# Out product, residual and norm of cross-attention in 28 tiles of 128 rows, and the first context load moved

## What is computed

```python
x = layernorm(x + self_attention(x))            # 16 heads of 32, causal
q = x @ Wq.T + bq; k = ctx @ Wk.T + bk; v = ctx @ Wv.T + bv
x = layernorm(x + softmax(q @ k.T) @ v)         # one head of 512
c = scan over the 16 batches of a gated recurrence (sigmoid, sigmoid, tanh)
x = layernorm(x + tanh(x @ wo.T + c_final @ uo.T + bo))
```

## Time and profile before

| | |
|---|---|
| median of 3 runs | 1415.57 us |
| profiled execution | 1416.02 us, span 1414.1 us |
| TensorE busy | 1385.4 us (98%), mean granted clock 0.994 |
| VectorE, ScalarE, GpSimd busy | 921.9, 731.6, 569.7 us |
| DMA | 157.94 MB, 37.8% of 16 engines' time |
| self-attention | about 0 to 385 us |
| cross-attention | about 385 to 837 us, 28.5 us per batch in the middle |
| recurrence and output gate | about 837 to 1414 us |

### The profile page before, as it was taken

The page is one execution under the profiler, slowest core; times in us unless marked ns, Lnnn a source line. Parts: engine busy times, 40 slices in busy tenths (PEclk is TensorE's granted clock), DMA queues, the critical chain, the costliest instruction groups (busy, mean ns, idle before and its releaser), DMA issues.

```text
span 1414.1 us, 28483 instructions
## 1 busy us (share of the span) xinstructions
PE 1385.4 (98%) x10017; PEld 1211.0 (86%) x10017; DVE 921.9 (65%) x1911; ACT 731.6 (52%) x1989; POOL 569.7 (40%) x475
## 2 busy tenths in 40 slices
PE   7999999999999999999999999999999999999997
PEld 4677777777789999999999988999999999999775
DVE  4589989999657756776677663345453444536697
ACT  4488888888565566656665655222232222222232
POOL 2476767676476565656565620000000000010264
PEclk9999999999999999999999999999999999999999
DMA  7014323335366675667567953010010100000353
GB/s 212 25 56 107 104 75 81 104 104 156 109 172 215 200 240 182 204 195 233 188 205 213 210 155 112 1 27 13 13 26 0 26 13 19 31 1 31 101 186 123
DMA packets 133079, 157.94 MB, mean 112 GB/s; under 512 B 62304, under 2 KB 70496, under 8 KB 133008
## 3 DMA queue, kind: packets, MB, share of 16 engines
q1 hardware_dynamic: 133008, 157.01, 37.8%
HBM read 105.61 MB, written 35.78 MB: 100 GB/s over the span
## 4 chain that ended last, share of the span: by engine, by line
PE 64%; issue 3%; POOL 3%; DMA 1%; DVE 1%; ACT 1%; POOLq 0%; ACTq 0%; DVEq 0%
PE banks L1522 16%; PE banks L1551 11%; PE banks L1007 9%; PE banks L1023 8%; PE banks L1036 6%; PE banks L1553 6%; PE banks L992 5%; POOL o_r L2097 1%; PE banks L977 1%; DMA s_cx_raw<-in_cx 1%; PE banks L1983 1%; PE banks L1053 1%; POOL o_rstd L2105 1%; POOL x_cx_lo L1367 1%; PE banks L2014 0%
## 5 line engine op out<-in xcount | busy, mean ns | idle before, releaser
L461 ACT ACTIVATE s_p<-banks,a_nmax 112x224 f32<-112x224 f32 (+1 forms) x512 | 198.1, 412 | 60.0 <-DVE a_nmax L572 59.9
L759 POOL TENSOR_TENSOR s_p<-s_p,a_rinv 112x896 f32<-112x896 f32 (+1 forms) x128 | 164.5, 1306 | 118.9 <-DVE a_rinv L580 115.8
L1496 POOL CAST m_hi<-w_raw 128x2048 fp32r<-128x2048 f32 x1 | 2.3, 2266 | 407.8 <-PE banks L1522 407.8
L1639 ACT ACTIVATE f_gate<-f_gate 128x448 f32<-128x448 f32 x90 | 52.2, 580 | 198.6 <-DVE f_gate L1762 198.6
L1759 DVE TENSOR_TENSOR f_gate<-banks,f_xg_early 128x448 f32<-128x448 f32 x45 | 28.1, 624 | 189.6 <-PE banks L1553 189.6
L1367 POOL TENSOR_TENSOR x_cx_lo<-s_cx_raw,x_cx_hi 125x512 fp32r<-125x512 f32 x96 | 120.8, 1296 | 37.0 <-ACT x_cx_hi L1136 37.0
L571 DVE TENSOR_REDUCE a_nmax<-banks 112x1 f32<-112x224 f32 x256 | 97.9, 382 | 24.5 <-PE banks L277 23.7
L461 ACT ACTIVATION_READ_ACCUMULATOR s_p<-banks,a_nmax 112x1 f32 x512 | 111.6, 218 | 0.0
L294 PEld LDWEIGHTS banks<-identity,s_p 112*112 112x112 f32 x768 | 88.0, 134 | 21.8 <-issue 2.3
L294 PE MATMUL banks<-identity,s_p 112*112 112x112 f32 x768 | 105.4, 261 | 1.2 <-POOL s_p L759 0.7
L1360 POOL TENSOR_TENSOR s_ct<-s_ct_raw,s_ct 128x750 fp32r<-128x750 f32 x60 | 98.6, 1669 | 0.0
(11 more groups left out here) (255 smaller groups left out, 3727.5 us busy)
## 6 DMA issues: line engine op xcount, KB each, us to landing
s_ct_raw<-in_ct SPq DMA_DIRECT2D x16, 1500.0 KB, 6.7
s_cx_raw<-in_cx SPq DMA_DIRECT2D x16, 1500.0 KB
a_xt<-in_xt SPq DMA_DIRECT2D x16, 448.0 KB, 6.3
a_xrow<-in_x SPq DMA_DIRECT2D x16, 448.0 KB, 5.9
a_xres<-in_x SPq DMA_DIRECT2D x16, 448.0 KB, 6.7
x_scratch<-a_xn SPq DMA_DIRECT2D x16, 448.0 KB, 3.3
x_scratch<-x_xn SPq DMA_DIRECT2D x16, 448.0 KB, 4.6
x_halves<-x_halves SPq DMA_DIRECT2D x16, 448.0 KB, 3.2
```

The costliest lines, as they stand in the source:

```text
L461: e = act.activation((p1 if c else p0)[:, g, h, :], src, ACT.Exp, bias=nmax[:, g % 2, c, h:h + 1], accum_out=rsum[:, g % 2, c, h:h + 1])
L759: pool.tensor_tensor(p[:, g, :, :], p[:, g, :, :], inv, ALU.mult).then_inc(norm_done, 1)
```

## The change

Four batches are 896 rows, which is 7 tiles of 128. The out product, the residual, the norm and the stores of x2 and of its halves work on these tiles: after batch 0 of four (q = 0) one tile is complete, after batches 1, 2 and 3 two more each. `ot_hi` and `ot_lo` are 384 columns wide and hold the remainder of a batch until the next. The row sums' reciprocals are laid out by 112 rows and are needed by 128, so they are stored to memory and loaded back; the residual's rows are loaded from memory by 128 rows as well, and POOL adds the bias in place. All loops of the stage run over four batches instead of two.

```diff
 # tables and the two new loads (SP)
+        OF = ((0, 1), (1, 3), (3, 5), (5, 7))
+        SLOT = ((0,), (1, 2), (0, 1), (2, 0))
+        PUT = (((0, T, 0),), ((0, 160, T), (160, T, 0)), ((0, T, 64),), ((0, 96, 288), (96, T, 0)))
...
+            def inverse_rows(b, at, odd):
+                i, q = four(at)
+                wait(sp, rinv_stored, 16 * (b + 1))
...
+                    sp.dma_start(rinv_rows[:, odd, 0:rows(at)], rinv_dram[i][128 * OF[q][0]:128 * OF[q][1]].rearrange("(n p) -> p n", p=128))\
+                      .then_inc(rinv_in, 16)
+            def residual_rows(b, at):
+                wait(sp, rinv_done, b + 1)
...
+                    sp.dma_start(rinv_scratch[b].rearrange("(c p) -> p c", p=R), rinv[:]).then_inc(rinv_stored, 16)
+                wait(sp, r_done, TC * b)
+                sp.dma_start(x1b[:, 0:rows(at), :], tiles_of(x1_rows, at)).then_inc(x1b_in, 16)
...
+            def loads(b, odd, at=None):
+                i, q = four(b if at is None else at)
+                if within(b - 2, B):
+                    inverse_rows(b - 2, (i, q - 2), odd)
...
+                residual_rows(b - 1, (i, q - 1))
 # out product (PE)
-                for c in rows:
+                for c in some[0:n]:
+                    slot = slice(128 * SLOT[q][c], 128 * SLOT[q][c] + 128)
...
-                            mm = pe.matmul(ps_h[0:R, c, :], y[:, k, c * R:c * R + R], w[:, k, :],
-                                           start=(i == 0), stop=(i == 3 * KC - 1))
+                            mm = pe.matmul(ps_h[:, c, :], y[:, k, slot], w[:, k, :], start=(i == 0), stop=(i == 3 * KC - 1))
 # exponentials (ACT): x1th(b + 1) goes between the two halves
+                    if c == 1 and within(b + 1, B) and not (isinstance(b, int) and b == 0):
+                        x1th(b + 1)
...
-                if within(b + 1, B) and not (isinstance(b, int) and b == 0):
-                    x1th(b + 1)
 # residual (DVE)
+                wait(dve, rinv_in, 16 * (b + 1))
 # bias of the residual (POOL)
-                wait(pool, x1_in[odd], 16 * (i + 1))
-                wait(pool, r_done, TC * (b - 1))
+                wait(pool, x1b_in, 16 * (b + 1))
...
+                if within(b - 1, B):
+                    residual_bias(b - 1, (i, q - 1))
                 if within(b, B):
                     cxl(b)
 # self-attention's SP: the first context load stands ahead of the loop over batches 4 to 13
+            sp.dma_start(shared.ct_raw[:], io["ct"][0].rearrange("(k p) t -> p k t", p=128)).then_inc(shared.ct_in, 16)
+            sp.dma_start(shared.cx_raw[:], io["cx"][0].rearrange("(c p) d -> p c d", p=XR)).then_inc(shared.cx_in, 16)
             with sp.Fori(2, B // 2 - 1) as i:
...
             step(B - 2, B % 2)
-            sp.dma_start(shared.ct_raw[:], io["ct"][0].rearrange("(k p) t -> p k t", p=128)).then_inc(shared.ct_in, 16)
-            sp.dma_start(shared.cx_raw[:], io["cx"][0].rearrange("(c p) d -> p c d", p=XR)).then_inc(shared.cx_in, 16)
```

More of the change, by code:

```diff
@@ L948, in sync @@
                 loads(b, b % 2)
[L949 to L952, removed]
+            with sp.Fori(1, B // 4 - 1) as i:
+                for q in range(4):
+                    loads(4 * i + q, q % 2, (i, q))
+            for b in range(B - 4, B - 1):
+                loads(b, b % 2)
             for i, name in enumerate(("wi_t", "wf_t")):
@@ L1074, in step, with separate @@
                 if isinstance(b, int) and b == B - 1:
-                    out(b - 1, range(0, 1))
+                    out(b - 1, b - 1, range(0, 1))
                 elif within(b - 1, B):
-                    out(b - 1)
+                    out(b - 1, (i, q - 1))
             for b in range(4):
[L1080 to L1085, removed]
+                step(0, b)
+            with pe.Fori(1, B // 4 - 1) as i:
+                for q in range(4):
+                    step(i, q)
+            for b in range(B - 4, B + 1):
+                step(b // 4, b % 4)
             for t in range(6):
                 next_input(t)
-        def separate(act, b):
+        def separate(act, b, at=None):
+            n = rows(b if at is None else at)
             wait(act, xn_done, TC * (b + 1))
             wait(act, halves_stored, 16 * b)
-            act.activation(halves[:], xn[:].bitcast(U16).rearrange("p c (d w) -> p c w d", w=2), ACT.Copy).then_inc(halves_done, 1)
+            act.activation(halves[:, 0:n, :, :], xn[:, 0:n, :].bitcast(U16).rearrange("p c (d w) -> p c w d", w=2), ACT.Copy)\
+               .then_inc(halves_done, 1)
         def scalar(act):
@@ L1129, in oth @@
                     wait(act, ot_done, 2 * b + half + 1)
-                    act.activation(ot_hi[:, 2 * half:2 * half + 2, :], ps_g[:, half, 0:2 * T], ACT.Copy).then_inc(oth_done, 1)
+                    for first, end, place in PUT[q]:
+                        a = act.activation(ot_hi[:, 2 * half:2 * half + 2, place:place + end - first], ot_columns(half, first, end), ACT.Copy)
+                    a.then_inc(oth_done, 1)
             def cxh(b):
@@ L1138, in exp @@
             def exp(b):
+                if isinstance(b, int) and b == 0:
+                    act.wait_ge(shared.xn_done, TC * B)
                 wait(act, pt_done, XC // 2 * b)
@@ L1193, in scalar @@
             x1th(1)
-            act.wait_ge(shared.xn_done, TC * B)
-            for b in range(2):
-                step(b)
-            with act.Fori(2, B - 2) as b:
-                step(b)
-            step(B - 2)
-            step(B - 1)
-            step(B)
+            act.wait_ge(shared.r_done, TC * B)
+            for b in range(4):
+                step(0, b)
+            with act.Fori(1, B // 4 - 1) as i:
+                for q in range(4):
+                    step(i, q)
+            for b in range(B - 4, B + 1):
+                step(b // 4, b % 4)
             next_columns(0)
@@ L1266, in statistics @@
+            def statistics(b, at):
+                n = rows(at)
+                each = TC // n
+                for c in range(n):
+                    wait(dve, r_done, TC * b + each * (c + 1))
+                    dve.bn_stats(stats[:, c, :], r[:, c, :]).then_inc(stats_done, each)
+                for c in range(n):
                     dve.wait_ge(pad_done, 1)
-                    wait(dve, stats_done, TC * b + c + 1)
-                    dve.bn_aggr(mv[:, c, :], stats[:, c, :]).then_inc(mv_done, 1)
@@ L1313, in step @@
                 if within(b - 1, B):
-                    residual(b - 1, 1 - odd, range(0, 1) if isinstance(b, int) and b == B - 1 else range(TC))
-                if within(b, B) and not (isinstance(b, int) and b == B - 1):
+                    residual(b - 1, (i, q - 1), range(0, 1) if isinstance(b, int) and b == B - 1 else range(TC))
+                if within(b, B):
                     inverse(b)
@@ L1385, in gpsimd @@
             for b in range(4):
[L1386 to L1391 removed]
+                step(0, b)
+            with pool.Fori(1, B // 4 - 1) as i:
+                for q in range(4):
+                    step(i, q)
+            for b in range(B - 4, B + 2):
+                step(b // 4, b % 4)
         opening.separate, opening.store = separate, store
```

238 lines of the change are left out of this document (131 added, 107 removed).

## The result

The changed kernel takes **1527.38 us** (median of 4 runs, 1525.30 to 1529.19) against 1415.39 before: 1.0785 times, 95% interval 1.0763 to 1.0807. That is 112 us more, where 32 were forecast, and outside the range.

The account below looks back on a forecast made before the run. TensorE, busy 98% of the span, was taken to bound the kernel, with a ring through the DMA queue near its limit. 1416.0 + 19 (cross-attention) + 13 (self-attention) = 1448 us, range 1420 to 1466.

Parts of the forecast that it names:

- the standstill in self-attention: Self-attention, batch 5: columns land late behind the moved context load, POOL held 15 us, TensorE idle 12; +13 us (9 to 17).
- the gain: Out product in cross-attention: 28 tiles of 128 rows instead of 32 of 112, 48 products fewer, 11.2 us saved.
- the ring through the residual's rows: Cross-attention: next context load waits for POOL's subtractions, these for the bias, that for the residual's rows; 29.4 us a step.
- The forecast's second ring: Cross-attention: SP waits for the reciprocals' store, delaying transposed columns, ACT's rounding and exponential, then TensorE's transposes; 29.4 us.
- the slack: Cross-attention: transposes start 4.9 us after the context rows' issue, which was to carry the first two steps.
- the two weights: Cross-attention's last context load: two 1 MB weights ahead of it in the queue, no longer hidden; 5 us.
- the draining: Last step of cross-attention: POOL's subtractions end later; 3 us (0 to 4.9).
- The store is 224 values of 4 bytes: Cross-attention: the reciprocals' store behind `s_ahead` in the queue delays what follows by 0.3 us (0 to 1.1).
- Slower still: Rival: TensorE's clock falls in each step's wait, up to 1.7 us in 12 steps; 1468 us, chance 0.13.
- The faster rival: Rival: ring and standstill both hidden, residual's rows landing within 17.8 us of the context rows' issue; 1405 us, chance 0.09.
- The fit beside it: The skill's rule, one DMA takes 2.0 us plus bytes over 436 GB/s: halves would land after 3.1 us, not 11.8.
- the moved load: Self-attention: the first context load, now directly ahead of batch 5's columns in the queue, makes them late; +13 us.

Follow-up runs that it names:

- e5: The kernel before with only the first context loads of cross-attention issued ahead of self-attention's loop; 1429.86 us.
- e12: The kernel before with each context rows' load split in two, 112 and 13 of its 125 partitions; 1412.74 us.
- e8: e6 with each context rows' load split in two, 112 and 13 of its 125 partitions; 1401.18 us.
- e2: The change with the reciprocals copied from SBUF to SBUF, nothing of them through memory; 1453.08 us.
- e6: e2 with the first context loads back at their old place and POOL adding the bias behind the context's low parts; 1411.18 us.
- e1: The change without the reciprocals' store, load and waits, the product multiplied by 1.0 instead; 1454.11 us.
- e4: The change with each reciprocal stored as 4 bytes, 512 bytes from one address to the next; 1452.29 us.
- e9: The change with each reciprocal stored as 4 bytes, 64 bytes from one address to the next; 1453.62 us.
- e3: The change with each reciprocal stored with 127 zeros behind it, as one piece of 512 bytes; 1456.95 us.
- e11: The change with each store of reciprocals issued a second time, to another scratch; 1606.11 us.
- e10: The change with the two reciprocals of a partition stored side by side, 112 writes of 8 bytes a batch; 1472.16 us.

## Why the prediction was wrong

**Right: the standstill in self-attention**, +13 forecast, +14 measured alone (e5), with POOL held 15.42 us (15) and TensorE 12.2 (12) in the profile after.

**Right: the gain**, 11.2 us forecast, 10.8 to 11.6 between e12 and e8. It only appears once nothing else is in the way: by the context loads, a one-tile step takes 26.2 us in e8 against 28.5 in e12, and a two-tile step 28.5 in both.

**Right in its mechanism, too small in its size: the ring through the residual's rows.** The forecast has 19.4 + 2.4 + 7.55 + 0.1 = 29.4 us for every step. Without dense writes e2 shows 20.3 + 2.37 + 8.38 = 31.1 in a two-tile step (its context rows at 618.13, the rows below on POOL), and 27.5 to 29.3 in the one-tile steps, on average 30.16:

```profile
638.43 2.40 POOL L1426 TENSOR_TENSOR x_x1b<-x_x1b,s_bv_all 128x1024 f32<-128x1024 f32 x1 [10.31 <-DMA x_x1b<-x_scratch]
640.80 8.38 POOL L1440 TENSOR_TENSOR x_cx_lo<-s_cx_raw,x_cx_hi 125x512 fp32r<-125x512 f32 x6
```

e6 shows the mechanism: in cross-attention only POOL's order changed against e2, and the ring was gone. The forecast's second ring, through SP's wait for the store, wasn't the limit: e1 and e2 are without it and no faster than e4 and e9.

In time, cross-attention without the dense writes is 1453.1 - 1415.4 - 14 = +24 us; +19 was forecast, with 30 as the bound. That the two are so near is partly luck. By the context loads of e2 and before, the later twelve steps cost 21 us more (30.3 each against 28.5), where the forecast has 11, and the first two 9, where it lets the slack carry them. What follows the last context load is 2 us shorter, where the forecast adds 5 for the two weights and 3 for the draining: the step that holds the weights takes 30.7 us, no more than the two-tile steps before it.

**Wrong: "The store is 224 values of 4 bytes. I take 0.3 us (bounds 0 and 1.1)."** With its reading back it cost 5.0 us a step (35.20 less 30.16), 74 us in all (1527.4 less 1453.1), about seventeen times the value taken and over four times the bound; 4.1 of them lie in the store's own flight. I had bounded it by the nearest row that counts bytes, a 448 KB DMA, because no row of the kernel before shows a store of many small pieces side by side. A bound by bytes can't hold what isn't paid by the byte; and the store wasn't one DMA more in the queue, it slowed the DMAs that were in flight. Where such a store is free, the runs lie 4 to 9 us over the forecast's sum of 1448 and inside its range: e2, e3, e4 and e9 take 1452 to 1457.

**The rivals.** "Slower still" had the right sign and the wrong cause: the clock did fall (0.91 over 440 to 800), but behind waits that the writes made. TensorE's own work is 305.54 / 360 x 35.20 = 29.9 us a step there and 340.44 / 360 x 30.16 = 28.5 in e2, so at most 1.4 of the 5.0 us can be the clock's; whether these lie on the path stays open. The faster rival needed the residual's rows at 17.8 us; in e2 they are ready at 20.3. The fit beside it (the Trainium skill, DMA: Bandwidth & Descriptors, Anatomy of one DMA) is stated for DMAs that GpSimd issues, and here SP issues all of them; e2's halves, at 16.9 us, are as far from its 3.1 as those of rows 5.

One remark of the forecast's gain is wrong and moves nothing: both layouts have 3584 rows of output and none in padding; what falls is the number of tiles, by four.

**The parts of the 112 us:** 74 dense writes, 14 the moved load, 24 the ring less the gain. With a direct copy, the load at its old place and POOL's other order the kernel is at 1411, 5 under the one before in that round, since POOL's order alone gives back 28 (e6); with the context rows on all engines it is at 1401 (e8), 15 under.

## What to carry to other kernels

Values of one per partition that must change their partition can be copied from SBUF to SBUF, or stored with 64 bytes from one address to the next; stored side by side as 4-byte pieces they slowed everything that this core was transferring. When a load is added to a queue, don't ask only whether it lands in time, but what stands behind the instruction that waits for it: here one swap on POOL was worth 28 us. And before a new kind of operation is priced at a fraction of a microsecond by the nearest row, ask whether that row pays for the same thing (bytes, pieces, neighbours); where none does, the upper end of the range should be open.

## What the runs showed of the hardware

- 224 writes of 4 bytes to one stretch of 896 bytes in memory slow all transfers of the core, down to 27 GB/s for 4 us, and cost this kernel 5 us a time (e11 adds one such store and 5.6 us a step). At steps of 64 or 512 bytes the same writes cost nothing that can be told, and in pairs of 8 bytes 0.3 us of the 4.1 while they fly. Which part of the chip makes neighbours wait for one another, no run shows.
- A copy of single values from SBUF to SBUF, 3 or 4 DMAs for 224 values, costs nothing beside none (1453.08 against 1454.11 us).
- The reading back suffers as well: the load of the reciprocals, one 4-byte value per partition and tile, lands after 5.6 us in the change, 3.5 in e10 and 1.8 in e4 and e9 (medians for two tiles, 440 to 800). The transposed columns behind it land after 10.4, 9.5 and 7.8 to 7.9 us, and while it is in flight the core moves 9 GB/s for 2 us (672 to 674 in the change).
- Behind a DMA over 112 partitions and one over 13, what follows in the queue lands in about half the time that it takes behind one over 125: halves 6.0 us against 14.0, `s_ahead` 7.4 against 12.8 (e8, e6).
